# Width products copied whole by ScalarE, added from memory, and two height banks evicted by one engine each

## The reference

```python
attn = jnp.einsum('nqc,nkc->nqk', q, k) * scale
r_h = rel_pos_h[idx]
r_w = rel_pos_w[idx]
q4 = q.reshape(-1, WS, WS, HD)
bias_h = jnp.einsum('nhwc,hkc->nhwk', q4, r_h)
bias_w = jnp.einsum('nhwc,wkc->nhwk', q4, r_w)
attn = attn + bias_h[..., :, None] + bias_w[..., None, :]
attn = jax.nn.softmax(attn, axis=-1)
o = jnp.einsum('nqk,nkc->nqc', attn, v)
```

## Time and profile before

| | |
|---|---|
| median of 3 runs | 317.58 us (314.58, 317.58, 317.61) |
| the profiled execution | 314.28 us, its span 312.5 us |
| PE busy | 299.3 us, 96% of the span |
| DVE, ACT, POOL busy | 184.7, 137.5, 96.5 us |
| granted TensorE clock | 1.000 |
| relative products to first transposed scores, block 1 | 21.57 to 38.19 us |
| the same in block 2 | 169.04 to 185.46 us |

### The profile page before, as it was taken

One profiled execution on the slowest core, in us unless ns is written; L12 is line 12 of the kernel. 1 busy time (PEld: TensorE's weight loads), 2 busy tenths in 40 slices (PEclk: granted clock), 3 DMA queues, 4 the chain that ended last, 5 costly groups with the idle time before them and its releaser, 6 DMA issues.

```text
span 312.5 us, 9268 instructions
## 1 busy us (share of the span) xinstructions
PE 299.3 (96%) x3886; PEld 230.5 (74%) x3886; DVE 184.7 (59%) x433; ACT 137.5 (44%) x304; POOL 96.5 (31%) x213
## 2 busy tenths in 40 slices
PE   6899799999989999999999889999998999999996
PEld 3468698888765469968846878899876547997476
DVE  5757876877777101236874787687868510363572
ACT  3565256555654530023256625655566543012420
POOL 4002995226610096000000399423662022000000
PEclk9999999999999999999999999999999999999999
DMA  7993000000031030200031100000000000000003
GB/s 211 396 347 71 19 9 17 13 6 3 20 119 28 0 120 6 75 2 2 1 103 23 35 10 10 16 14 4 5 4 2 0 0 0 3 0 0 2 2 102
DMA packets 10236, 14.07 MB, mean 45 GB/s; under 512 B 3473, under 2 KB 8177, under 8 KB 10194
## 3 DMA queue, kind: packets, MB, share of 16 engines
q1 hardware_dynamic: 9570, 13.38, 13.5%
q10 hardware_dynamic: 624, 0.09, 0.2%
HBM read 11.21 MB, written 0.79 MB: 38 GB/s over the span
## 4 chain that ended last, share of the span: by engine, by line
PE 83%; DVE 11%; DMA 2%; ACT 2%; issue 1%; ACTq 0%; SPq 0%; DVEq 0%
PE banks L1148 14%; PE banks L1112 11%; PE banks L1245 11%; PE banks L1263 10%; PE banks L1168 6%; PE banks L1029 5%; DVE attention_arena L1713 3%; PE banks L998 3%; PE banks L1429 3%; PE banks L987 3%; PE banks L1276 2%; PE banks L1066 2%; PE banks L1323 2%; PE banks L1293 1%; PE banks L1350 1%; PE banks L1376 1%
## 5 line engine op out<-in xcount | busy, mean ns | idle before, releaser
L1527 ACT ACTIVATE arena<-banks 128x392 f32<-128x392 f32 (+1 forms) x112 | 48.9, 492 | 36.3 <-PE banks L1148 29.8
L1728 DVE TENSOR_REDUCE negmax<-banks 128x4 f32<-128x784 f32 (+1 forms) x48 | 46.0, 959 | 15.7 <-PE banks L1112 15.2
L1112 PE MATMUL banks<-attention_arena 32*128 32x196 f32 x384 | 49.0, 352 | 3.3 <-DVE attention_arena L1713 1.7
L1148 PE MATMUL banks<-attention_arena 32*128 32x196 f32 x384 | 47.2, 337 | 1.1 <-DMA attention_arena<-negmaxT 0.6
L1148 PE MATMUL banks<-attention_arena,keys 32*128 32x196 f32 x384 | 45.2, 324 | 0.0
L1112 PE MATMUL banks<-keys,attention_arena 32*128 32x196 f32 x384 | 44.2, 323 | 0.0
L1148 PEld LDWEIGHTS banks<-attention_arena 32*128 32x128 f32 x384 | 31.0, 184 | 6.3 <-issue 4.5
L1245 PE MATMUL banks<-yT,fc 128*128 128x512 f32 (+1 forms) x96 | 33.3, 607 | 0.0
L1112 PEld LDWEIGHTS banks<-attention_arena 32*128 32x128 f32 x384 | 29.1, 183 | 5.5 <-DVE negmax L1723 3.2
L1148 PEld LDWEIGHTS banks<-attention_arena,keys 32*128 32x128 f32 x384 | 32.9, 184 | 0.0
L1263 PEld LDWEIGHTS banks<-fc,arena 128*128 128x128 f32 x192 | 31.1, 190 | 1.5 <-ACT arena L1548 1.5
(11 more groups left out here) (197 smaller groups left out, 569.1 us busy)
## 6 DMA issues: line engine op xcount, KB each, us to landing
fc<-in_fc SPq DMA_DIRECT2D x2, 768.0 KB, 5.2
fc<-in_fc SPq DMA_DIRECT2D x2, 576.0 KB, 5.6
attention_arena<-negmaxT SPq DMA_DIRECT2D x68, 1.0 KB
rel<-in_rel SPq DMA_DIRECT2D x2, 448.0 KB, 5.1
x_tok<-in_x SPq DMA_DIRECT2D x4, 192.0 KB, 4.0
inverse<-in_inverse SPq DMA_DIRECT2D x1, 768.0 KB
inverse<-in_space_back SPq DMA_DIRECT2D x1, 768.0 KB, 4.2
qkv<-in_qkv SPq DMA_DIRECT2D x1, 576.0 KB, 4.1
```

The lines of the kernel that those rows point to most:

```text
L1112: ins = mm(o, asking, asked, start=not with_rel, stop=bool(with_rel))
L1148: last = mm(m.bank[turned_in(n, j)][key_rows(b), cols * tile:cols * (tile + 1)], keys_of(n, j, tile)[with_rel], queries_of(n, j, tile)[wit ...
L1527: run(m.probsT[keys, n % P_RING, j, 0:cols], m.bank[turned_in(n, j)][keys, 0:cols], ACT.Exp).then_inc(s.probs, 1)
L1728: dve.tensor_reduce(at[rows, 2 * tiles * part:2 * tiles * (part + 1)].rearrange("k (j a) -> k j a", a=tiles), m.banks[rows, 2 * part:2 * p ...
```

## The change

In three parts.

1. **Widths**: ACT copies a whole bank, both halves, into `m.relw` in one instruction of 512 columns, four in all; nobody else reads these banks. DVE adds half 1 from that copy, not from the bank, all four column groups for slot 0 first, then all four for slot 1 (`add_widths`). POOL adds half 0 to slot 2, as before, as soon as each copy is there.
2. **Heights**: banks 0 and 1 as before. Bank 2 is evicted by ACT alone (three instructions), bank 3 by DVE alone (three).
3. **Waits**: PE's first scores wait for ACT's four copies and DVE's four adds of slot 0. POOL's edge copies wait for all eight adds.

```diff
 PROJ += [("v", n, 0, "act") for n in range(2)]
-PROJ += [("rel_h", n, 0, "act") for n in range(REL_JOBS)] + [("rel_w", n, 0, "dve") for n in range(REL_JOBS)]
+PROJ += [("rel_h", n, 0, "act" if n < REL_JOBS - 1 else "dve") for n in range(REL_JOBS)] + [("rel_w", n, 0, "act") for n in range(REL_JOBS)]
...
-        m.relw2, _ = carve(arena, at, 128, REL_JOBS, AT_ONCE, IMAGES * SIDE)
+        m.relw, _ = carve(arena, at, 128, REL_JOBS, AT_ONCE, 2, IMAGES * SIDE)
...
-            return to, bank.rearrange("k (w s n) -> k s w n", w=AT_ONCE, s=2)[:, which]
+            return to, m.relw[:, g, :, which]
...
-                for n, g in enumerate(THIRDS):
-                    if n == 0:
-                        pool.wait_ge(s.rel_h2, REL_JOBS)
-                    pool.wait_ge(s.rel_w2, n + 1)
-                    to = m.r[:, 2].rearrange("k (n w) -> k w n", w=SIDE)[:, AT_ONCE * g:AT_ONCE * (g + 1)]
-                    pool.tensor_tensor(to, to, m.relw2[:, g], ALU.add).then_inc(s.rel_added, 1)
+                for g in range(REL_JOBS):
+                    if g == 0:
+                        pool.wait_ge(s.rel_h2, REL_JOBS - 2)
+                        for last in range(REL_JOBS - 2, REL_JOBS):
+                            wait_for(pool, s.proj_in, *taken_out(job("rel_h", last, 0)))
+                    wait_for(pool, s.proj_in, *taken_out(job("rel_w", g, 0)))
+                    to, of = products(job("rel_w", g, 0), 0)
+                    pool.tensor_tensor(to[:, 2], to[:, 2], of, ALU.add).then_inc(s.rel_added, 1)
                 pool.wait_ge(s.rel_added, REL_JOBS)
-                pool.wait_ge(s.proj_in.dve, taken_out(job("rel_w", REL_JOBS - 1, 0))[1])
+                pool.wait_ge(s.rel_w2, 2 * REL_JOBS)
...
                     elif kind == "rel_h":
                         to, of = products(j, 1)
-                        if g == REL_JOBS - 1:
-                            act.wait_ge(s.rel_h2, THIRDS.index(g) + 1)
+                        one = c["slot_cols"][:, 2 * SLOTS:2 * SLOTS + 1]
                         for slot, mask in enumerate((UPPER, LOWER)):
...
+                        if g == REL_JOBS - 2:
+                            to, of = products(j, 0)
+                            ins = run(to[:, 2], of, ACT.Identity, bias=one)
                     elif kind == "rel_w":
-                        third = job("rel_w", THIRDS[g], 0)
-                        act.wait_ge(s.proj_in.pe, produced(third))
-                        if THIRDS[g] < REL_JOBS - 1:
-                            act.wait_ge(s.proj_in.dve, taken_out(third)[1])
-                        run(m.relw2[:, THIRDS[g]], products(third, 0)[1], ACT.Copy).then_inc(s.rel_w2, 1)
-                        continue
+                        ins = run(m.relw[:, g].rearrange("k w s n -> k (w s n)"), bank[:, :], ACT.Copy)
...
+                def add_widths(slot, g):
+
+                    j = job("rel_w", g, 0)
...
+                    wait_for(dve, s.proj_in, *taken_out(j))
+                    mask = (LOWER, UPPER)[slot]
+                    to, of = products(j, 1)
+                    dve.scalar_tensor_tensor(to[:, slot], of, c["slot_cols"][:, mask:mask + 1], to[:, slot], ALU.mult, ALU.add).then_inc(s.rel_w2, 1)
...
                 for j, (kind, g, part, who) in enumerate(PROJ):
-                    if who == "dve" or kind == "rel_h":
+                    if who == "dve" or kind == "rel_h" and g < REL_JOBS - 2:
                         take_job(j)
+                for slot in range(2):
+                    for g in range(REL_JOBS):
+                        add_widths(slot, g)
```

More of the change, by code:

```diff
@@ L64 @@
 REL_JOBS = SIDE // AT_ONCE
-THIRDS = (0, 1, 3, 2)
 HALF_COLS = SIDE // 2 + 1
@@ L1010, in open_bank @@
                     if PROJ[j - 8][0] == "rel_h":
-                        pe.wait_ge(s.rel_h2, THIRDS.index(PROJ[j - 8][1]) + 1)
+                        pe.wait_ge(s.rel_h2, PROJ[j - 8][1] + 1)
                 return m.bank[job_bank(j)]
@@ L1471, in attention @@
                 for j, (kind, g, part, who) in enumerate(PROJ):
-                    if who != "act" and kind != "rel_w":
+                    if who != "act":
                         continue
@@ L1485, in attention @@
                         to, of = products(j, 1)
-                        if g == REL_JOBS - 1:
-                            act.wait_ge(s.rel_h2, THIRDS.index(g) + 1)
+                        one = c["slot_cols"][:, 2 * SLOTS:2 * SLOTS + 1]
                         for slot, mask in enumerate((UPPER, LOWER)):
-                            ins = run(to[:, slot], of, ACT.Identity, scale=c["slot_cols"][:, mask:mask + 1], bias=c["slot_cols"][:, 2 * SLOTS:2 * SLOTS + 1])
+                            ins = run(to[:, slot], of, ACT.Identity, scale=c["slot_cols"][:, mask:mask + 1], bias=one)
+                        if g == REL_JOBS - 2:
+                            to, of = products(j, 0)
+                            ins = run(to[:, 2], of, ACT.Identity, bias=one)
                     elif kind == "rel_w":
-                        third = job("rel_w", THIRDS[g], 0)
-                        act.wait_ge(s.proj_in.pe, produced(third))
-                        if THIRDS[g] < REL_JOBS - 1:
-                            act.wait_ge(s.proj_in.dve, taken_out(third)[1])
-                        run(m.relw2[:, THIRDS[g]], products(third, 0)[1], ACT.Copy).then_inc(s.rel_w2, 1)
-                        continue
+                        ins = run(m.relw[:, g].rearrange("k w s n -> k (w s n)"), bank[:, :], ACT.Copy)
                     elif kind == "v":
@@ L1698, in take_job @@
                     elif kind == "rel_h":
-                        third = job("rel_h", THIRDS[g], 0)
-                        dve.wait_ge(s.proj_in.pe, produced(third))
-                        if THIRDS[g] < REL_JOBS - 1:
-                            dve.wait_ge(s.proj_in.act, taken_out(third)[1])
-                        to, of = products(third, 0)
-                        dve.tensor_scalar(to[:, 2], of, c["slot_cols"][:, 2 * SLOTS:2 * SLOTS + 1], None, ALU.add).then_inc(s.rel_h2, 1)
-                        return
-                    else:
-                        if g == 0:
-                            dve.wait_ge(s.proj_in.act, taken_out(job("rel_h", REL_JOBS - 1, 0))[1])
+                        one = c["slot_cols"][:, 2 * SLOTS:2 * SLOTS + 1]
+                        to, of = products(j, 0)
+                        if who == "act":
+                            wait_for(dve, s.proj_in, *taken_out(j))
+                            dve.tensor_scalar(to[:, 2], of, one, None, ALU.add).then_inc(s.rel_h2, 1)
+                            return
+                        dve.tensor_scalar(to[:, 2], of, one, None, ALU.add)
                         to, of = products(j, 1)
-                        if g == REL_JOBS - 1:
-                            dve.wait_ge(s.rel_w2, THIRDS.index(g) + 1)
-                        for slot, mask in enumerate((LOWER, UPPER)):
-                            ins = dve.scalar_tensor_tensor(to[:, slot], of, c["slot_cols"][:, mask:mask + 1], to[:, slot], ALU.mult, ALU.add)
+                        for slot, mask in enumerate((UPPER, LOWER)):
+                            ins = dve.tensor_scalar(to[:, slot], of, c["slot_cols"][:, mask:mask + 1], one, ALU.mult, ALU.add)
                     ins.then_inc(s.proj_in.dve, 1)
+                def add_widths(slot, g):
+                    j = job("rel_w", g, 0)
+                    if slot == g == 0:
+                        for last in range(REL_JOBS - 2, REL_JOBS):
+                            wait_for(dve, s.proj_in, *taken_out(job("rel_h", last, 0)))
+                    wait_for(dve, s.proj_in, *taken_out(j))
+                    mask = (LOWER, UPPER)[slot]
+                    to, of = products(j, 1)
+                    dve.scalar_tensor_tensor(to[:, slot], of, c["slot_cols"][:, mask:mask + 1], to[:, slot], ALU.mult, ALU.add).then_inc(s.rel_w2, 1)
                 def take_max(h):
```

## The result

The changed kernel takes 318.59 us, median of 17 runs (316.7 to 320.21); the kernel before, run beside it, 315.86, median of 17 (314.29 to 318.29). The ratio is 1.0076, 95% interval 1.0052 to 1.0100: **slower by 0.8%, some 2.4 us.** The profiled execution took 320.21 us, the highest of its runs, as that of before, 314.28, stands at the low end of its own.

What follows compares the result with a forecast made beforehand. PE, busy 96%, bounds the kernel; only its stands can give time, clocked by DVE's first maximum. Held adds make that 1.2 us late in two blocks: 314.28 plus 2.4 gives 316.7 us, range 313.3 to 320.0.

Steps and rivals of the forecast that it cites:

- The sum: Both blocks: first maximum 1.2 us late each, 2.4 in all, added to the profiled 314.28 us: 316.7 us.
- The hold: DVE's slot 0 adds from SBUF and POOL's adds block each other; first maximum 0.7 to 1.7 us late per block; chance 0.48.
- The turn: One DVE add and one POOL add taking turns on a width bank: 1.13 to 1.39 us, four turns per block.
- Reading L1660 as evidence: A normalisation from SBUF ended 0.11 us after POOL's instruction, so it was taken as held; it has one tensor input.
- Rival 1: No hold at DVE's adds: first maximum 0.6 us early, block 1 perhaps 0.3; 1.0 in all, 313.3 us; chance 0.33.
- Rival 2: DVE's and POOL's adds exclude each other for whole records, 1.57 us a turn; 4.8 us slower, 319.1 us; chance 0.10.
- rival 3: First maximum does not move: two held turns or adds 0.15 us slower use up the 0.6; 314.3 us; chance 0.09.
- Memory as a source at the bank's price: DVE's width adds reading the SBUF copy follow one another after 0.57 us, as when reading the bank.
- The copy: ACT's copy of a 512-column width bank takes 0.60 us, between rows of 0.38 and 0.68.
- Heights at nothing: ACT's and DVE's height instructions end before the first copied width bank arrives, so they were costed at nothing.
- POOL's edge copies delay nothing: Six of twelve edge copies after DVE's last add take 1.07 us; maxima's transpose comes 1.96 after the first maximum.
- SP's queue: Block 1: SP issues value rows until 34.99 us, so less than the 0.6 us gain may come through.

Runs made afterwards that it cites:

- experiment 6: Changed kernel with DVE's eight adds made one-input multiply-adds from memory, four variants; no kernel time given; the first variant's adds took 1022 to 1127 ns beside POOL.
- the fills: Changed kernel with POOL's four adds to slot 2 replaced by zero fills, which read nothing; no kernel time given, first maxima at 9.68 and 9.62 us.
- experiment 4: Changed kernel with slot 0's four DVE adds reading the bank again after ACT's copy, slot 1's still from memory; 315.95 us, ratio 0.9976 to the kernel before.
- the three runs with columns: Changed kernel with DVE's adds made one-input, factor and addend read from columns: original layout, even dimensions, odd dimensions; no kernel times given.
- widths-alone kernel: Kernel before with only the widths copied whole and added from memory, slot 0 first, heights as before; 318.87 us, ratio 1.0096.
- the odd run: Changed kernel with DVE's adds made one-input over 255 elements, 5 x 51 in, 3 x 85 out; no kernel time given, 939 to 1044 ns beside POOL.

## Why the prediction came out as it did

- **The sum, its last step, is what failed.** The mechanism and its size, 2.4 us, were right; I put them on the profiled execution (314.28 + 2.4 = 316.7) although the runs shown had a median 3.3 above it, and so wrote a number below the kernel's own median, as if the change did nothing or gained. The other sum of the same sentence, 320.0 on the median of three runs, erred to the other side. Seventeen runs put the median of before at 315.86; with 2.4 that is 318.3, and 318.59 was measured. The range, 313.3 to 320.0, holds it, and so does "no change" within 1%; its sign was not to be had from 316.7. The level lies in the start of the program: its first height varies by 3.1 us between profiles, more than the whole effect, with TensorE's pace in the first projection. The profile that I built on has none of the slow matmuls there, and so stands at the low end of its kernel's runs. That 1% is about what a measurement can tell was wrong as well: seventeen runs each tell 0.8% from nothing, to 0.25% either way.
- **The hold** (0.48): shown. Adds over 1 us, POOL's 1.2 apart, first maximum 1.14 and 1.16 late where 1.2 was said. The turn is 1.21 by POOL's starts and 1.23 by DVE's, between the bounds 1.13 and 1.39. *The Trainium skill ("SBUF — State Buffer", section "Who interferes with whom") has a VectorE instruction with two SBUF inputs and a reading GpSimd block each other: these adds agree, DVE's with 1.26 to 1.36 us for 0.69, POOL's with 1.24 to 1.26 for 0.87.*
- **Reading L1660 as evidence** The earlier trace rows was sound, for a reason that I then did not have: it has one input, and so had the held instructions of experiment 6. Rival 1 (0.33) is what the fills show, 0.54 and 0.62 early for the 0.6 worked out. Rival 2 (turn 1.57) and rival 3 did not occur.
- **Memory as a source at the bank's price**: right, 0.58 against 0.57. *The 65 ns per add that I worked out from the Trainium skill ("VectorE: DVE Perf Modes", TRN2 errata) as an estimate are not there.*
- **The copy**: 0.60 said, 0.60 measured. First add 4.23 after the first height; the prediction's 26.88 is 4.09. (Its 0.1 us between PE and ACT is 0.04 by its own two rows, 31.14 after 31.10.)
- **Heights at nothing**: wrong in a small way. Alone they bring 0.26 and 0.28 us, as ACT no longer waits for DVE in front of bank 3's heights (0.43 us) and DVE's first add starts at 4.15 in place of 4.41; with the copies behind them some 0.6.
- **POOL's edge copies delay nothing**: right. In block 2 the chain goes by all twelve of them to SP, but six of them release the transfers, and those ended at 187.48, before the maxima's transpose at 188.27; the last copy (188.52) ends after SP had begun (188.35). The chain names the copies here by their time alone.
- **SP's queue**, named as a limit on block 1's gain, is one, and can take more than the gain: experiment 4.

## What to carry to other kernels

Before an operand is moved from a bank to memory to free the bank, look at what GpSimd does in those microseconds: in this kernel VectorE's two-input adds from memory and GpSimd's adds take turns, at some 1.2 us for a pair of 128x256, one-input multiply-adds are held too, and for the two-input adds one operand in a bank avoids it altogether. Put a difference in microseconds on the median of the runs, never on the one profiled run, and measure stages in two profiles from a common instruction just ahead of the change. A stage made earlier gains only up to the next queue behind it, here SP's, and a wait that it opens on TensorE can cost clock as well.

## What was not expected of the hardware

- A one-input VectorE instruction from memory to memory is held beside GpSimd's add (0.40 us alone, 0.94 to 1.05 held), even with 5 x 51 elements in and 3 x 85 out. Not all are: in the profile of before the transpose of 128x768 and the reduction of 128x576, both from memory, ran beside GpSimd's edge instructions and took 0.94 and 0.73 us, in the profile after too. No run has them alone, but this is 1.22 and 1.27 ns an element, where the one-input instruction alone goes at 1.25 (0.32 us for 256). What tells the two kinds apart stays open. *The Trainium skill ("VectorE: DVE Perf Modes", the section on the mode with both read ports) gives one-source instructions from SBUF a second port only where the outer dimensions are even or equal; the odd run speaks against this as the whole reason, if the chip takes its two shapes as they are written.*
- With two inputs on VectorE both engines' records stretch (0.69 to 1.26 and more, 0.87 to 1.24); with one input only VectorE's does (GpSimd 0.85 to 0.93 in the three runs with columns).
- After 2.31 to 3.21 us without work TensorE's granted clock fell to between 0.58 and 0.83 in the next windows, part of them at 1.2 GHz (pairs of score matmuls 0.33 us apart in place of 0.17); the three profiles with it lost 1.5 to 1.6 us before block 2. In the widths-alone kernel, whose profile has no record of the clock, the score matmuls behind a stand of 1.80 us took what they took before (0.61 and 0.54 us a group).
